# A decoder layer's attention loop: contexts' halves and row statistics moved between steps

## The reference

```python
x = x + attention(layernorm(x), Wq, Wk, Wv, Wo, bo)     # 8 batches, 256 tokens, 512 features
x = x + long_convolution(ctx, ctx, layernorm(x), ssm_kernel, D, head_dim=8)
x = x + ternary_ffn(layernorm(x), w_gate_up, w_proj)
```

## Time and profile before

| what | value |
|---|---|
| median of 3 runs | 1187.93 us (1187.45 to 1189.96) |
| the profiled execution | 1186.55 us, span 1184.8 us |
| TensorE busy | 1131.4 us, 95% |
| VectorE, GpSimd, ScalarE busy | 881.1, 687.7, 553.0 us |
| attention batches 1 to 6 | 78.6 to 80.7 us each |

### The profile page before, as it was taken

The page is one execution under the profiler, slowest core; times in us unless marked ns, Lnnn a source line. Parts: engine busy times, 40 slices in busy tenths (PEclk is TensorE's granted clock), DMA queues, the critical chain, the costliest instruction groups (busy, mean ns, idle before and its releaser), DMA issues. The chain is left out here.

```text
span 1184.8 us, 27046 instructions
## 1 busy us (share of the span) xinstructions
PE 1131.4 (95%) x10882; PEld 810.0 (68%) x10882; DVE 881.1 (74%) x1287; ACT 553.0 (47%) x617; POOL 687.7 (58%) x557
## 2 busy tenths in 40 slices
PE   4998999989999999999899999999999999999998
PEld 4665566747657667576576677777886876786683
DVE  6979778787888787888877788888745645654654
ACT  6866564653755655637555500000244543542441
POOL 1454394784865947848659589999342422423331
PEclk9998999999999999999999999999999999999999
DMA  9463444563455355634455357783001022013000
GB/s 325 152 210 108 121 132 118 166 173 118 124 160 174 105 142 157 186 113 141 132 174 156 146 114 144 146 145 83 1 19 44 11 55 54 17 36 54 19 19 36
DMA packets 166183, 134.15 MB, mean 113 GB/s; under 512 B 69628, under 2 KB 127362, under 8 KB 166082
## 3 DMA queue, kind: packets, MB, share of 16 engines
q1 hardware_dynamic: 141128, 126.44, 37.3%
q10 hardware_dynamic: 24960, 6.29, 3.6%
HBM read 81.76 MB, written 35.21 MB: 99 GB/s over the span
## 5 line engine op out<-in xcount | busy, mean ns | idle before, releaser
L701 PE MATMUL bank<-hT_halves,w_hi 128*128 128x256 f16 x640 | 176.6, 276 | 13.5 <-DMA hT_halves<-parts 8.3
L1984 POOL TENSOR_TENSOR parts<-parts 128x512 f32<-128x512 f32 x80 | 118.2, 1480 | 107.6 <-DVE parts L1446 107.6
L702 PE MATMUL bank<-hT_halves,w_hi 128*128 128x256 f16 x640 | 176.3, 276 | 0.0
L703 PE MATMUL bank<-hT_halves,w_lo 128*128 128x256 f16 x640 | 176.3, 275 | 0.0
L963 PE MATMUL bank<-kv,toep 128*128 128x288 f32 (+2 forms) x660 | 157.8, 401 | 0.7 <-ACT qT L1211 0.5
L963 PEld LDWEIGHTS bank<-kv,toep 128*128 128x128 f32 x660 | 123.7, 190 | 34.0 <-ACT qT L1211 0.7
L2002 POOL TENSOR_TENSOR ctx_lo<-ctx,ctx_hi 128x512 f16<-128x512 f32 x64 | 105.7, 1652 | 67.2 <-ACT ctx_hi L1153 67.1
L1989 POOL TENSOR_SCALAR_AFFINE_SELECT region_c<-region_c 128x512 f32<-128x512 f32 x128 | 106.2, 854 | 60.2 <-ACT region_c L1177 60.2
L2132 POOL TENSOR_TENSOR sqsum<-sqsum,toep 128x512 f32<-128x512 f32 x56 | 78.1, 1395 | 95.4 <-ACT toep L1353 95.2
L1174 ACT ACTIVATE region_c<-bank,cap_scale 128x1536 f32<-128x1536 f32 x64 | 98.7, 1542 | 63.0 <-PE bank L782 62.9
L1041 PE MATMUL bank<-odd_halves,guT 128*128 128x256 f16 x512 | 112.2, 273 | 0.0
(11 more groups left out here) (192 smaller groups left out, 2633.9 us busy)
## 6 DMA issues: line engine op xcount, KB each, us to landing
unit_halves<-halves SPq DMA_DIRECT2D x80, 256.0 KB, 2.2
q_both<-unit_halves SPq DMA_DIRECT2D x64, 256.0 KB, 2.9
q_high<-unit_halves SPq DMA_DIRECT2D x64, 128.0 KB, 3.0
toep<-kernel_padded SPq DMA_DIRECT2D x32, 256.0 KB, 4.1
wffn<-w_gu SPq DMA_DIRECT2D x6, 1280.0 KB, 6.2
cpair<-ctx_pairs SPq DMA_DIRECT2D x32, 176.0 KB, 4.7
xin<-x SPq DMA_DIRECT2D x8, 512.0 KB, 3.8
region_o<-wq SPq DMA_DIRECT2D x4, 1024.0 KB, 11.5
```

The source lines that it names most:

```text
L701: pe.matmul(dst, lh, rh, start=first and k == 0, stop=False)
L702: pe.matmul(dst, lh, rl, start=False, stop=False)
L703: mm = pe.matmul(dst, ll, rh, start=False, stop=last and k == n - 1)
L1984: pool.tensor_tensor(slot[:, 0], slot[:, 0], slot[:, 1], ALU.add).then_inc(unit_summed, 1)
```

## The change

ScalarE: `high_ctx(b, step - 3)` moves ahead of `soften` and `take_values` of its step; the rounding of the next batch's rows moves from step 7 to step 6. VectorE: in the loop, the statistics of x2 (steps 5 and 6 before) and `prepare(b + 1)` (step 6 before) move to step 1; `prepared` and the rows' low halves move from step 7 to 6. GpSimd: `low_ctx` of group step - 3, not step - 4, now behind `add_keys` and ahead of `add_parts`; `keep_x2` and `deviation` move from step 7, ahead of the mask, to step 1, behind it. TensorE's and SyncE's lists stay.

```diff
--- before.py
+++ after.py
@@ -1180,13 +1180,13 @@
                 for step in range(STEPS):
                     if step == CUT_SLOT:
                         act.wait_ge(quant_step, QUANT_STEPS * (b - 1) + DIGITS)
+                    if step >= 3:
+                        high_ctx(b, step - 3, False)
                     if step < NG:
                         soften(b, step)
                     if step < TT:
                         take_values(b, step)
-                    if step >= 3:
-                        high_ctx(b, step - 3, False)
-                    if step == 7:
+                    if step == 6:
                         for i in range(TT):
                             act.wait_ge(ln_done, TT * (b + 1) + i + 1)
                             act.activation(row_halves[:, i, 0], xin[:, i, :], ACT.Copy, scale=ACT_SCALE).then_inc(hT_hi_done, 1)
@@ -1614,11 +1614,11 @@
                         low_unit(b, EARLY + step - 2)
                     if 4 <= step < 6:
                         scale_digits(b - 1, step - 3)
-                    if 5 <= step < 5 + TT:
-                        statistics_of_x2(step - 5, 2 * TT * b)
+                    if step == 1:
+                        for i in range(TT):
+                            statistics_of_x2(i, 2 * TT * b)
+                        prepare(b + 1, 2 * TT * b + TT)
                     if step == 6:
-                        prepare(b + 1, 2 * TT * b + TT)
-                    if step == 7:
                         prepared(b + 1)
                         for i in range(TT):
                             dve.wait_ge(hT_hi_done, TT * (b + 1) + i + 1)
@@ -2009,18 +2009,18 @@
 
             def attend(b):
                 for step in range(STEPS):
-                    if step >= 4:
-                        low_ctx(b, step - 4)
                     if 1 <= step < NG + 1:
                         add_keys(b, step - 1)
+                    if step >= 3:
+                        low_ctx(b, step - 3)
                     if 2 <= step < 2 + LATE:
                         add_parts(b, EARLY + step - 2)
-                    if step == 7:
+                    if step < NG:
+                        mask(b, step)
+                    if step == 1:
                         keep_x2(b - 1, 4 * TT * b + 2 * TT)
                         deviation(b + 1, 4 * TT * b + 4 * TT)
-                    if step < NG:
-                        mask(b, step)
-                for g in range(STEPS - 4, NG):
+                for g in range(STEPS - 3, NG):
                     low_ctx(b, g)
                 for n in range(EARLY):
                     add_parts(b + 1, n)
```

## The result

The changed kernel takes 1213.16 us in the median of 4 runs (1210.37 to 1215.54), the kernel before 1188.88 us in the same comparison: the ratio is 1.0218, 95% interval 1.0189 to 1.0246. The change makes the kernel some 25 us slower. The forecast was 1198 us, slower by 10.5 us, with 1205 us as the upper end of its range; the direction was right, the size was not.

A forecast was written before the change was run, and what follows sets the result against it. TensorE's queue and its stops bound the kernel, with L1594 setting when rows land. Five batches at 2.4 us late, 1.0 for batch 6 and -2.5 for the last gave +10.5 us: median 1198 us, range 1183 to 1205.

The forecast's parts named there:

- What bounds the loop: TensorE's queue plus stops, 95% busy; VectorE's product L1594 gates weight store, loads and transposes, and TensorE resumes 16.9 us later.
- (a): Statistics in VectorE's step 1: product L1590 meets GpSimd's work, so add_parts(7) comes 1.8 us late, without slack.
- (b): low_ctx(0) ahead of add_parts(8) on GpSimd: add_parts(8) and (9) 2.8 us late, L1594 2.1 to 2.7, 2.4 taken.
- (c): High contexts ahead of tanh on ScalarE: tanh of group 3 starts later, adding a 0.35 us stop to TensorE.
- (d): TensorE's stops in batch 3: 1.5 us removed, 1.8 added, all covered by some 3 us of waiting for rows.
- the sum: Whole kernel: 5 x 2.4 + 1.0 - 2.5 = +10.5 us on 1186.55, giving 1197.05 profiled, 1198 as median.
- (e): Rows' halves in step 6: no gain where the queue is busy; batch 6 wins back up to 2.5 us, +1.0 taken.
- (f): Last batch: little delayed, three ctx_lo stops go, some 3.7 us in all, of which 2.5 us counted as gain.
- the first (rows land by their issue): Transposes land soon after issue and both kinds of TensorE waits go: 1167 us profiled, 1168.5 median; chance 0.12.
- the second (the delay vanishes in idle time): L1594 doesn't move; only batch 6 and the last batch gain: 1182.7 us, median 1184; chance 0.15.
- The third (ScalarE's rows in step 6 hold TensorE up): Rows ahead of tanh of group 7 wait for VectorE, so TensorE arrives after the rows: 1207 us; chance 0.05.

## Why the prediction was wrong in size

Its steps, in its order:

- **What bounds the loop** was right. The landing of the rows starts each batch, and L1594 sets it. The first transpose lands 1.0 to 1.2 us behind the residual in every batch of both kernels, however early it is issued.
- **(a) and (b)** were right in mechanism and nearly in size. Forecast: L1594 2.1 to 2.7 us late, 2.4 taken; measured 2.68. GpSimd's add_parts(8) and (9) came 2.7 us late where 2.8 was worked out. Of the parts, statistics cost 1.8 and contexts 0.9 by themselves. One premise of (a) was off: the mask of group 1, held up by L1590 before, was said to be awaited by nobody, but add_keys(1) started right behind it.
- **(c) and (d)** had TensorE's stops right: 0.34, 0.33 and 0.90 us where 0.3, 0.35 and 1.15 were forecast, all hidden by the wait for the rows. The wait in batch 3 was 3.10 us, as forecast. But batch 3 was not typical: the six waits were 2.5 to 5.9 us, 4.2 in the mean.
- **The step that failed is what (d) and the sum made of that longer wait.** "This changes nothing", says (d), and in the sum a batch costs what L1594 is late and nothing more. A wait of 3 to 6 us also costs what follows it: TensorE is granted 1.2 GHz at its end and behind it. The stretch from landing to the next find_below grew by 1.28 us a batch, 7.7 us in the loop, and filling the wait with matmuls took 7 to 8 us off. The sum had no term for it. The Trainium skill, page "TensorE: Matmul & The Clock Gate", section Part 1: The HAM clock gate, says that an idle TensorE falls back to the lower of its two clocks and pays for it when work returns; the windows above agree (0.57 to 0.65 of the full clock over the 4 us behind the wait).
- **(e)** The queue decided, as forecast, and rows in step 7 instead of 6 made no difference in time. But the landing came 0.47 us later in the mean, 2.8 us in the loop, a term that the sum lacked too. Of the 0.47, the residual's own landing makes 0.33: the loads were issued 5.24 us behind L1594 instead of 4.73, most of all in batches 4 and 6, where the last store landed 6.1 us behind L1594 instead of 4.3 to 4.4 (in batch 2 of the kernel before it was 6.15). The first transpose's distance from the residual makes 0.10, the second's distance from the first 0.04. Why stores and transposes landed as they did isn't known. Batch 6 was misread: there too the first transpose landed 1.15 us behind the residual, before the change, and it was the second that came 3.5 us behind the first. I counted on a gain of up to 2.5 us; its landing went from 17.86 to 19.29.
- **(f)** The last batch was to give 2.5 us. From its find_below to the end it took 571.2 us before and 572.4 us after. Of this, one further fall of the clock near 862 us, in the part that the change doesn't touch, is some 1.7, an estimate: half of its 3.4 us. The ctx_lo stops, 3.7 us, went, and TensorE waited instead for the x2 tiles and their copies (1.3 and 1.5 us), more than the 1.2 that I had set against them. Another 1.1 us were lost ahead of the loop, where the change does nothing.

Put together on the profiled spans: 16.1 (L1594, six batches of 2.68) + 2.8 (landing) + 7.7 (behind the landing, the clock) = 26.6 us in the loop, and 2.4 us outside it, against a forecast of 13.0 and -2.5. The sum is 18.5 us short: 7.7 for the clock, 4.9 outside the loop, 2.8 for the landing, 1.7 for L1594's size, 1.4 for the gain of batch 6 that didn't come. The right direction was no luck, as L1594 and the queue did what was forecast.

Of the rivals, the first (rows land by their issue) and the second (the delay vanishes in idle time) are refuted by the landing and by L1594. The third (ScalarE's rows in step 6 hold TensorE up) is not borne out: with the rows back in step 7 the time is the same.

## What to carry to other kernels

Before an operation is moved, look at what it pushes, not only at what it costs. Here 3.8 us of statistics made the critical product L1594 1.8 us late, by pushing another product from one of GpSimd's operations onto a later one; and one context operation of 1.2 us, put ahead of add_parts instead of behind it, cost L1594 1.8 us in the changed kernel. Follow each move down to the one instruction that starts the long DMA chain. And when a forecast makes the busiest engine wait longer than it ever did before, give the wait a second term: the clock behind it.

## What the runs showed of the hardware

- TensorE's granted clock fell to 1.2 GHz, for 3.4 or 6.8 us, at every wait for the rows of 2.9 us or more in any of the kernels here, during the wait or within 1.4 us behind its end. At waits of 2.1 to 2.9 us it fell in some cases (2.16 us with the statistics alone, 2.33 us with the residual behind the transposes on the kernel before) and not in others (2.82 us in the kernel before, 2.54 us in the changed one). Matmuls of no use in the wait of the changed kernel kept it up.
- A bfloat16 tensor_tensor of VectorE and an operation of GpSimd took turns: GpSimd's tensor_tensor of 1.27 us became 3.05 or 3.06 us and its mask of 1.22 us 3.02 us, and the product itself took 3.0 to 3.1 us where it had to wait in its turn.
- Two DMA transposes of 128 x 1024 float16 with no load ahead of them landed 2.8 and, in five of six batches, 4.3 us after the first one's issue; behind a queued load about 1 and 1.9 us after that load. The second sometimes came 2.3 us or more behind the first (batches 1 and 6 of the changed kernel, and 3.5 us in batch 6 of the kernel before); why isn't settled.
